# Table sums in high and low parts: twelve of sixteen steps instead of eight, with rings of three buffers

## The reference

```python
q = (x @ Wq).reshape(b, n, HEADS, DIM) * DIM ** (-0.5)
kv_scores, indices = _pk(x, Wq_pk, pk_keys)
offsets = jnp.arange(HEADS, dtype=indices.dtype) * NUM_KV
ind = indices + offsets[None, None, :, None]
k = jnp.einsum('bnhk,bnhkd->bnhd', kv_scores, keys_table[ind])
v = jnp.einsum('bnhk,bnhkd->bnhd', kv_scores, values_table[ind])
sim = jnp.einsum('bihd,bjhd->bhij', q, k)
...
attn = jax.nn.softmax(sim, axis=-1)
out = jnp.einsum('bhij,bjhd->bhid', attn, v)
```

## Time and profile before

| | |
|---|---|
| median of 3 runs | 2220.28 us (2218.65 to 2233.55) |
| profiled execution, its own time | 2221.55 us |
| its span in the trace | 2219.7 us |
| TensorE busy | 2111.7 us (95%) |
| VectorE, ScalarE, GpSimd busy | 1688.8, 1566.5, 1264.6 us |
| table sums, ordinary (L991), of the chain that ended last | 26% |
| table sums, split (L999 and L1003), of that chain | 14% and 7% |
| log weights (L982) of that chain | 15% |

### The profile page before, as it was taken

The page is one execution under the profiler, slowest core; times in us unless marked ns, Lnnn a source line. Parts: engine busy times, 40 slices in busy tenths (PEclk is TensorE's granted clock), DMA queues, the critical chain, the costliest instruction groups (busy, mean ns, idle before and its releaser), DMA issues.

```text
span 2219.7 us, 45163 instructions
## 1 busy us (share of the span) xinstructions
PE 2111.7 (95%) x12240; PEld 1527.6 (69%) x12240; DVE 1688.8 (76%) x5126; ACT 1566.5 (71%) x3250; POOL 1264.6 (57%) x1300
## 2 busy tenths in 40 slices
PE   5994869999999999999999999999999999999997
PEld 4882547777777767777777677777777677777775
DVE  4554468888888888888888788888888888888885
ACT  3653347777777777777777777777777777777775
POOL 2430136666666666666666666666666666666664
PEclk9996869999999999999999999999999999999998
DMA  2000020000000010001000100000000100010000
GB/s 90 1 0 0 1 93 6 4 6 24 28 6 6 6 45 5 5 6 45 7 6 6 45 5 5 6 20 31 6 6 6 45 5 5 6 45 7 6 6 16
DMA packets 16603, 37.36 MB, mean 17 GB/s; under 512 B 6048, under 2 KB 14496, under 8 KB 15261
## 3 DMA queue, kind: packets, MB, share of 16 engines
q1 hardware_dynamic: 13746, 36.03, 5.3%
q10 hardware_dynamic: 2795, 0.70, 0.1%
HBM read 24.40 MB, written 0.70 MB: 11 GB/s over the span
## 4 chain that ended last, share of the span: by engine, by line
PE 84%; DVE 1%; issue 1%; ACT 1%; DMA 0%; DVEq 0%; POOL 0%; SPq 0%; ACTq 0%; POOLq 0%
PE ps L991 26%; PE ps L982 15%; PE ps L999 14%; PE ps L1003 7%; PE ps L1036 5%; PE ps L1054 3%; PE ps L962 2%; PE ps L1026 2%; PE ps L1020 2%; PE ps L975 2%; PE ps L1046 2%; PE ps L1037 1%; PE ps L1013 1%; DVE k_W L1445 0%; ACT k_W L1161 0%
## 5 line engine op out<-in xcount | busy, mean ns | idle before, releaser
L1326 POOL TENSOR_TENSOR k_W_low<-k_W,k_W_high 128x688 fp32r<-128x688 f32 x513 | 852.0, 1661 | 497.0 <-ACT k_W_high L1166 497.0
L1445 DVE SCALAR_TENSOR_TENSOR k_W<-ps,k_W 128x688 f32<-128x688 f32 x1028 | 887.6, 864 | 323.9 <-ACT k_W L1161 314.3
L1161 ACT ACTIVATE k_W<-ps 128x688 f32<-128x688 f32 x1029 | 766.7, 745 | 465.1 <-PE ps L982 450.0
L991 PE MATMUL ps<-k_W,k_tab 128*128 128x344 f32 x2048 | 676.8, 453 | 0.0
L982 PE MATMUL ps<-k_X,k_sel 128*128 128x344 f16 x2058 | 476.1, 313 | 16.4 <-DVE k_W L1445 9.2
L991 PEld LDWEIGHTS ps<-k_W,k_tab 128*128 128x128 f32 x2048 | 366.7, 190 | 127.3 <-issue 0.5
L1166 ACT ACTIVATE k_W_high<-k_W 128x688 fp32r<-128x688 f32 x513 | 396.1, 772 | 0.0
L999 PE MATMUL ps<-k_W_high,k_tab_high 128*128 128x344 f32 x1024 | 385.2, 379 | 0.0
L999 PE MATMUL ps<-k_W_high,k_tab_low 128*128 128x344 f32 x1024 | 324.4, 319 | 0.0
L982 PEld LDWEIGHTS ps<-k_X,k_sel 128*128 128x128 f16 x2058 | 142.3, 98 | 236.3 <-issue 99.3
L1003 PE MATMUL ps<-k_W_low,k_tab_high 128*128 128x344 f32 x1024 | 244.4, 320 | 0.0
(11 more groups left out here) (221 smaller groups left out, 2786.0 us busy)
## 6 DMA issues: line engine op xcount, KB each, us to landing
k_tab<-in_tables SPq DMA_DIRECT2D x9, 2048.0 KB, 7.2
k_xq<-x2T SPq DMA_DIRECT2D x66, 86.0 KB, 2.0
k_xs<-x2T SPq DMA_DIRECT2D x66, 86.0 KB, 2.0
cst<-in_consts SPq DMA_DIRECT2D x1, 1024.0 KB, 18.5
wts<-in_weights SPq DMA_DIRECT2D x1, 896.0 KB, 12.7
cst<-in_consts SPq DMA_DIRECT2D x1, 874.5 KB, 16.2
xr<-in_xrows SPq DMA_DIRECT2D x1, 750.0 KB
xT<-in_xcols SPq DMA_DIRECT2D x1, 750.0 KB, 14.6
```

The costliest lines, as they stand in the source:

```text
L991: mm = mm_(sums, tab[:, slot, at + k, :], W[:, d % RING, k, :], start=(d == 0 and k == 0), stop=(d == NDC - 1 and k == 1))
L1161: A(W[:, d % RING, :, :], ps[:, 2 * (d % 2):2 * (d % 2) + 2, 0:LOUT], ACT.Exp).then_inc(e_done, 1)
L1326: G.tensor_tensor(W_low[:, q % SPLIT_RING, :, :], W[:, d % RING, :, :], W_high[:, q % SPLIT_RING, :, :].bitcast(F32), ALU.subtract).then_i ...
L1445: V.scalar_tensor_tensor(W[:, d % RING, :, :], ps[:, 2 * (d % 2):2 * (d % 2) + 2, 0:LOUT], 0.0, W[:, d % RING, :, :], ALU.is_ge, ALU.mult) ...
```

## The change

Three of every four steps are split (d % 4 in 1, 2, 3) instead of two (1, 3). So steps 2, 6, 10 and 14 of each item turn from ordinary into split. The rings of high and low weights shrink from four buffers to three, and `table_high` and `table_low` make three chunks at a time instead of two. Nothing else in the text of the kernel differs.

```diff
-        SPLIT = (1, 3)
+        SPLIT = (1, 2, 3)
         SPLITS = [d for d in range(NDC) if d % 4 in SPLIT]
         NSPLIT = len(SPLITS)
         NPART = 2 * NSPLIT // 8
-        FIRST_ROW = (2, 6)
-        RING, SPLIT_RING = 8, 4
+        FIRST_ROW = (2, 5)
+        RING, SPLIT_RING = 8, 3
```

## The result

The changed kernel took 2326.48 us (median of 4 runs, 2322.55 to 2338.65) beside 2226.55 us for the kernel before (4 runs): ratio 1.0459 [1.0399, 1.0519]. Its profiled execution has a span of 2322.8 us, 103.1 more than the 2219.7 of the one before. I had forecast 75 + 2. The first 290 us, the token mixer's, come out some 12 us longer in some executions of any of these kernels (the first clamp ends at 290 to 295 us, or at 304 to 307), which widens the medians and leaves the items as they are.

A forecast was written before the change was run, and what follows sets the result against it. TensorE bounds the kernel (29.31 of 29.36 us an item), with the other engines near their limit. Per item +0.84 - 0.22 + 0.55 = +1.17 us, +75 over 64 items, +2 ahead: 2297 us, slower by 3.4%; range 2215 to 2330.

The forecast's parts named there:

- 75 + 2: Whole run: +1.17 us an item over 64 items gives +75; larger table parts ahead of the items give +2.
- Stretch 1: Slots 14 to 3: savings of 0.44 us lost; `floors` waits for GpSimd's low part, so slot 3 comes 0.84 later.
- Stretch 2: Slots 4 to 8: step 6's saving of 0.22 us is kept, with slack of 0.3 for step 10's weights.
- rivals 2 and 3: No `floors` delay: either nothing is delayed, 2208 us, chance 0.07, or only the `k_PT` copies are, 2243 us, 0.09.
- Stretch 3: Slots 8 to 13: step 10's saving of 0.22 us lost; ScalarE's `k_PT` copies end late, costing 0.55 an item.
- rival 3: The port at `floors` costs nothing, the `k_PT` copies do: +23 us, 2243 us; chance 0.09.
- rival 4: The port at `floors` costs, the `k_PT` copies don't: +42 us, 2262 us; chance 0.17.
- The ring of three: High parts with three buffers: waiting for the table sum of step d-4 instead of d-8 costs nothing.
- rival 5: Slot 6: `chosen` also meets GpSimd instructions, TensorE loses perhaps 0.5 to 1 us an item: 2330 to 2360; chance 0.10.

The follow-up runs named there:

- pe_alone: Kernel before, with table sums of steps 2, 6, 10, 14 as six float32r matmuls on the preceding step's parts, no work added elsewhere: 2201.34 us, ratio 0.9908.
- floors_single: Changed kernel with `floors` as six operations over 128x1 in place of two over 128x3: 2293.61 us, ratio 1.0317.
- floors_pt: Changed kernel with both the one-element `floors` and the `k_PT` copies moved ahead of the high part: 2259.51 us, ratio 1.0151.
- pt_first: Changed kernel with ScalarE's `k_PT` copies ahead of step 15's high part, `table_high` and `table_low` one slot later: 2358.97 us, ratio 1.0605.
- small_a: Changed kernel with TensorE's program 12 instructions shorter, leaving out waits that an earlier one covers: 2325.14 us, ratio 1.0474.

## Why the prediction came out

**Stretch 1, +0.84: right, and its cause shown.** Measured 0.84. L1419 went from 0.403 to 1.236 us (forecast about 1.2), ends with the second low part, and TensorE idles 1.12 us ahead of slot 3. That the savings of steps 14 and 2 are lost there was right but for 0.11 of 0.44: so much arrives in pe_alone, in which no other engine is touched. The Trainium skill (SBUF — State Buffer, section Who interferes with whom) says that VectorE's two-port modes and GpSimd share a port pair; floors_single agrees as far as that goes: an operation of 128x3 stands 1.24 us, one of 128x1 never (0.144). That the operation of 128x3 runs in such a mode, no run shows; that it ends with GpSimd's instruction, all do.

**Stretch 2, -0.22: right.** Measured -0.22. The clamp ends at 918.62, 4.92 us after the stretch began, the weights of step 10 at 919.86, and slot 7 starts at 920.15: the slack of 0.3 is there. But it is there only behind the late slot 3. With `floors` out of the way slot 6 loses 0.28 us (floors_single) to 0.38 (floors_pt) against the changed kernel, so rivals 2 and 3, which kept the 0.22 with `floors` out of the way, were priced too low.

**Stretch 3, +0.55: the mechanism right, the size 0.08 too small.** Measured +0.63, and all of it in slot 13 (2.63 to 3.26). The wait for L1196 is the 0.35 of the text; the start behind it costs 0.28, where I had estimated 0.2. The 0.18 on VectorE ahead of slot 11 is the lost saving of slot 10, which takes 1.58 us before and after, as forecast.

**The two as separate terms: wrong in kind.** The sum adds 0.84 and 0.55, and for the change as a whole that is what came. But rivals 3 and 4 priced the one without the other, and so did the expectations of floors_single and pt_first. Taking `floors`' delay away alone gave 0.56, not 0.84 (rival 3: 0.70 above the kernel before, priced at 0.33); taking the copies' delay away alone gave 0.12, not 0.55 (rival 4: 1.14 above it, priced at 0.62). I had argued each stretch from its own rows and not asked who sets the next one's start: GpSimd's row sets the end of `floors` and that of the clamp, so a TensorE that comes earlier to either only waits.

**The ring of three: free, as argued.** ScalarE had no idle time ahead of a high part in the whole run:

```profile
L1166 ACT ACTIVATE k_W_high<-k_W 128x688 fp32r<-128x688 f32 x770 | 601.2, 781 | 0.0
```

**The sum, +75 + 2: short by 26 of 103 us.** 6 are the 0.09 an item and 3 lie in the first two items. Of the +2 ahead of the items, VectorE's part is there: its eight pieces of L1519 take 3.83 us instead of 2.76. The time at which the first clamp ends (2.8 less) can't tell, since it lies anywhere from 290 to 307 us in these kernels. 21 are a term that the sum lacks: nothing in the text asks what the 64 added matmuls and weight loads do to the program of TensorE itself. The kernel before had 14 packets of q8 and no stop on issue, so its trace did not show the price; it did show the queue, with 0.23 MB. The section of the Trainium skill named under small_a has the store's size, and I had not weighed it: the loop over two heads is 1538 instructions before and 1614 after, by its blocks of 256 instructions 6.0 and 6.3 of the eight (an estimate), and more than six blocks on end can lie in eight. It would have been a reason to look, not a price: pe_alone's loop has 1602 and no long turn. The time of 2326 lies inside the range only because rival 5, which hardly happened (`chosen` took 266 ns at the median, over 0.6 us in 6 of 195 cases), had pulled its end up to 2330.

## What to carry to other kernels

When TensorE is 99% busy and yet every log weight waits with its weight load, a shorter matmul saves a part at best (0.33 of 0.88 us here, even with the work on the others left out); look for the ring first. When work goes to GpSimd, list VectorE's small operations from SBUF to SBUF inside GpSimd's new row, and give those on the path one element a partition. And count what a change adds to an unrolled loop on each engine: the packets of the instruction queue, and a wait on "issue" at the loop's turn, show when it has outgrown what is kept (here no long turn with a loop of 1538 instructions, three with 1614 and more, and none, one or three between). A slack that is read behind a delay goes with the delay: the 0.29 us ahead of slot 7 were there only while slot 3 was late.

## What the runs showed of the hardware that I had not expected

- 96 more instructions in TensorE's loops, none of them waited for, cost 23 us: three stops on issue of 23.5 us together, the longest 8.1, with 27 packets of 16 KB more. Two kernels of equal length (3710 instructions) can differ in it.
- An operation of VectorE over 128x3 in SBUF can lose to GpSimd several times over: 0.16 us alone, 1.24 behind one low part, 4.07 behind a gapless row; in all 64 long cases of the changed kernel it ends within 0.04 us of a GpSimd instruction's end. The same arithmetic as three operations of 128x1 takes 0.144 us each in all 195 cases.
- Two edits that save 0.56 us an item and, in the ordinary items alone, 0.12 save 1.08 together (floors_single, pt_first, floors_pt).
